# Retention rounds of a hybrid image and token network: absolute weights summed in pairs by GpSimd

## What is computed

```python
q, k = theta_shift(xn @ Wq), theta_shift(xn @ Wk)
qk = einsum("bhld,bhmd->bhlm", q, k * scaling) * mask      # 1024 x 1024 for each head
qk = qk / clip(sum(abs(qk), -1), 1, 50000)                 # row sums of absolute weights
out = einsum("bhlm,bhmd->bhld", qk, v)
out = layernorm(out) * ln_g + ln_b ; out = gelu(out) @ Wo
```

## Time and profile before

| what | value |
|---|---|
| median of 3 runs | 4394.82 us |
| lowest and highest run | 4376.67 and 4406.17 us |
| the profiled execution | 4402.8 us, its span 4401.0 us |
| mean granted TensorE clock over the span | 0.842 |
| busy over the span: PE, DVE, ACT, POOL | 72%, 62%, 40%, 35% |
| busy slices 2 to 10 of 40 (the retention stage): PE | 90% and more |

### The profile page before, as it was taken

The page is one execution under the profiler, slowest core; times in us unless marked ns, Lnnn a source line. Parts: engine busy times, 40 slices in busy tenths (PEclk is TensorE's granted clock), DMA queues, the critical chain, the costliest instruction groups (busy, mean ns, idle before and its releaser), DMA issues.

```text
span 4401.0 us, 50008 instructions
## 1 busy us (share of the span) xinstructions
PE 3157.9 (72%) x13837; PEld 1506.0 (34%) x13839; DVE 2724.1 (62%) x3838; ACT 1738.6 (40%) x3383; POOL 1533.5 (35%) x1297
## 2 busy tenths in 40 slices
PE   1899999999946637661576778757787877766648
PEld 0222222222213226651455556423343433333322
DVE  2678787788837779999655555304353443544467
ACT  0587887777835525440343444321111111100000
POOL 0111121111003458996423220253534435444500
PEclk9999999999966659995677777778988989888878
DMA  6544234442211127761011010110000000000014
GB/s 213 139 130 121 56 108 120 132 122 46 85 58 62 67 87 230 214 205 63 29 34 31 25 35 12 42 42 19 21 26 20 24 19 15 12 3 4 4 48 181
DMA packets 247369, 319.59 MB, mean 73 GB/s; under 512 B 52301, under 2 KB 183437, under 8 KB 246681
## 3 DMA queue, kind: packets, MB, share of 16 engines
q1 hardware_dynamic: 217496, 296.77, 22.1%
q0 software_dynamic: 29696, 20.97, 2.7%
HBM read 170.95 MB, written 146.67 MB: 72 GB/s over the span
## 4 chain that ended last, share of the span: by engine, by line
PE 27%; another core or an unknown queue 15%; issue 9%; DVE 9%; POOL 6%; ACT 3%; DMA 2%; SPq 0%; DVEq 0%; POOLq 0%; ACTq 0%
PE banks L1485 10%; POOL arena L903 4%; PE banks L1305 2%; PE banks L1476 2%; DVE arena L2405 2%; PE banks L1470 2%; PE banks L1365 1%; PE banks L1273 1%; ACT arena L1813 1%; DVE arena L2175 1%; POOL sorted_dram L890 1%; PE banks L1281 1%; POOL arena L916 1%; PE banks L1373 1%
## 5 line engine op out<-in xcount | busy, mean ns | idle before, releaser
L1485 PE MATMUL banks<-arena 128*128 128x512 f32 (+1 forms) x1920 | 797.2, 563 | 216.3 <-DVE arena L2586 177.1
L2586 DVE TENSOR_TENSOR arena<-arena,banks 128x1280 f32<-128x1280 f32 x320 | 465.0, 1484 | 665.6 <-remote 410.7
L1485 PEld LDWEIGHTS banks<-arena 128*128 128x128 f32 x1920 | 390.4, 205 | 682.8 <-issue 478.6
L2125 DVE TENSOR_TENSOR arena<-banks,arena 128x512 f32<-128x512 f32 x512 | 317.5, 681 | 105.2 <-PE banks L998 82.7
L812 POOL TENSOR_TENSOR pool_spare<-pool_spare 128x1 f32<-128x1 f32 x54 | 17.6, 326 | 1026.3 <-DVE edges_now L2551 717.6
L2125 DVE TENSOR_TENSOR keys<-banks,arena 128x512 f32<-128x512 f32 x512 | 317.5, 681 | 60.8 <-PE banks L998 39.0
L945 POOL DMA_INDIRECT arena<-src_dram,edges_now x336 | 317.4, 944 | 105.8 <-issue 105.8
L945 POOL DMA_INDIRECT arena<-dst_dram,edges_now x336 | 317.0, 943 | 102.4 <-issue 102.4
L2357 DVE TENSOR_TENSOR keys<-keys 128x2048 f32<-128x2048 f32 x132 | 345.7, 2658 | 2.3
L903 POOL TENSOR_TENSOR arena<-arena 128x256 f32<-128x256 f32 x144 | 337.3, 2376 | 21.8 <-ACT arena L1785 20.6
L1664 ACT ACTIVATE arena<-arena 128x512 f32<-128x512 f32 x512 | 286.8, 619 | 130.2 <-DVE arena L2125 88.5
(11 more groups left out here) (399 smaller groups left out, 5780.7 us busy)
## 6 DMA issues: line engine op xcount, KB each, us to landing
sorted_dram<-zeros SPq DMA_DIRECT2D x8, 8192.0 KB, 29.2
arena<-in_w SPq DMA_DIRECT2D x150, 384.0 KB, 4.0
arena<-parts_dram SPq DMA_DIRECT2D x192, 128.0 KB, 4.8
experts_dram<-keys SPq DMA_DIRECT2D x64, 256.0 KB
keys<-experts_dram SPq DMA_DIRECT2D x8, 2048.0 KB, 8.5
parts_dram<-nodes SPq DMA_DIRECT2D x16, 768.0 KB, 3.3
slot_out_dram<-arena SPq DMA_DIRECT2D x40, 256.0 KB, 4.4
arena<-sorted_dram SPq DMA_DIRECT2D x150, 64.0 KB, 3.3
```

Of the source, the lines that this page charges most:

```text
L1485: last = pe.matmul(banks[:, bank, 0:part.shape[1]], ohl[:, s, t, :], part, start=False, stop=False, skip_group_check=True)
L2125: dve.tensor_tensor(p_slots[r % 2][:, j, :], banks[:, j, :], table[:, PER_GROUP * g + j, at:at + HALF], ALU.mult).then_inc(masked, 1)
L2586: dve.tensor_tensor(rh[:, t % RH], oha[:, s, t:t + 1, :].broadcast_to([P, VALS, NB]), vals[:, t, :].unsqueeze(2).broadcast_to([P, VALS, NB ...
```

## The change

A new semaphore `paired` is counted by a new function of POOL. At every odd round POOL adds, head by head, the absolute tile of the even round before (`a_slots[0]`) into that of the odd round (`a_slots[1]`), in place. PE's `norm` runs only for odd rounds, and each of its four matmuls waits for its own addition and signals `norms` itself. It stands last in the index r even (after mix(r)), where it takes round r-1; the norm of round 31 stands in index 0 of the next image. ACT's Abs of an odd round waits for norm of two rounds ago, head by head; that of an even round waits for the addition of the round before, head by head. POOL's other work is put at fixed rounds behind the additions of that round, in a somewhat different order (`part_rest` before `divide` at r = 11). ACT's `part(n, 0, 1)` goes from r = 12 to 13. The semaphore `w4_in` is folded into `edges_in`, which changes no order.

```diff
@@ -249,6 +249,7 @@
         scores = sem("scores")
         masked = sem("masked")
         absolute = sem("absolute")
+        paired = sem("paired")
         norms = sem("norms")
         rot_added = sem("rot_added")
         part_step = sem("part_step")
@@ -399,7 +400,6 @@
         node_step = sem("node_step")
         vecB = sem("vecB")
 
-        w4_in = sem("w4_in")
         x3_in = [sem("x3_in_even"), sem("x3_in_odd")]
         gates_step = sem("gates_step")
         expert_ready = sem("expert_ready")
@@ -765,8 +765,8 @@
             for s in range(2):
                 load_norm(s, s)
             sp.wait_ge(rec_out, 32 * IMAGES)
-            sp.dma_start(rlast, src_dram[LAST_SRC:LAST_SRC + 1, :].broadcast_to([P, VALS])).then_inc(w4_in, 16)
-            sp.dma_start(select_in, t_in["select12"]).then_inc(w4_in, 16)
+            sp.dma_start(rlast, src_dram[LAST_SRC:LAST_SRC + 1, :].broadcast_to([P, VALS])).then_inc(edges_in, 16)
+            sp.dma_start(select_in, t_in["select12"]).then_inc(edges_in, 16)
 
             def store_experts(b):
                 for i in range(STEPS2):
@@ -837,34 +837,49 @@
                 pool.wait_ge(hn_rstd, m * (2 * PASSES) + (2 * p + 2))
                 pool.tensor_tensor(o_sb[:, p, :], o_sb[:, p, :], spread_sb[:, p % 2, :], ALU.mult).then_inc(hn_scaled, 1)
 
-            def retention(b, attend, head, tail):
-                if tail:
+            def add_pairs(b, r):
+                for j in range(PER_GROUP):
+                    pool.wait_ge(absolute, b * UNITS + r * PER_GROUP + (j + 1))
+                    pool.tensor_tensor(a_slots[1][:, j, :], a_slots[1][:, j, :], a_slots[0][:, j, :], ALU.add).then_inc(paired, 1)
+
+            def beside(b, r, attend, head, tail):
+                if r == 3 and tail:
                     divide(b - 1, 3)
                     scale_rows(b - 1, 2)
-                if head:
+                if r == 5 and head:
                     rotate_add(b + 1, 0, 0)
-                if head:
+                if r == 9 and head:
                     rotate_add(b + 1, 0, 1)
-                if attend:
-                    divide(b, 0)
-                if tail:
-                    scale_rows(b - 1, 3)
-                if head:
-                    part_rest(b + 1, 0, 0)
+                if r == 11:
+                    if head:
+                        part_rest(b + 1, 0, 0)
+                    if attend:
+                        divide(b, 0)
+                    if tail:
+                        scale_rows(b - 1, 3)
+                if r == 13 and head:
                     part_rest(b + 1, 0, 1)
-                if head:
+                if r == 17 and head:
                     rotate_add(b + 1, 1, 0)
-                if attend:
+                if r == 19 and attend:
                     divide(b, 1)
                     scale_rows(b, 0)
-                if head:
+                if r == 21 and head:
                     rotate_add(b + 1, 1, 1)
+                if r == 23 and head:
                     part_rest(b + 1, 1, 0)
-                if head:
-                    part_rest(b + 1, 1, 1)
-                if attend:
-                    divide(b, 2)
-                    scale_rows(b, 1)
+                if r == 27:
+                    if head:
+                        part_rest(b + 1, 1, 1)
+                    if attend:
+                        divide(b, 2)
+                        scale_rows(b, 1)
+
+            def retention(b, attend, head, tail):
+                for r in range(ROUNDS):
+                    if attend and r % 2:
+                        add_pairs(b, r)
+                    beside(b, r, attend, head, tail)
 
             for n in range(2):
                 for h in range(HALVES):
@@ -1014,13 +1029,12 @@
 
             def norm(b, r):
                 ps, a = divmod(r, BLOCKS)
-                if a == 0:
+                if a == 1:
                     since(pe, sum_step, b * (4 * PASSES) + (4 * ps - 3))
-                pe.wait_ge(absolute, b * UNITS + (r + 1) * PER_GROUP)
                 for j in range(PER_GROUP):
-                    last = pe.matmul(banks[ROWS * j:ROWS * (j + 1), 5, :], ones[:, 0:ROWS],
-                                     a_slots[r % 2][:, j, :], start=(a == 0), stop=(a == BLOCKS - 1))
-                last.then_inc(norms, 1)
+                    pe.wait_ge(paired, b * (UNITS // 2) + r // 2 * PER_GROUP + (j + 1))
+                    pe.matmul(banks[ROWS * j:ROWS * (j + 1), 5, :], ones[:, 0:ROWS],
+                              a_slots[1][:, j, :], start=(a == 1), stop=(a == BLOCKS - 1)).then_inc(norms, 1)
 
             def row_mean(m, p):
                 pe.wait_ge(o_ready, m * PASSES + (p + 1))
@@ -1143,13 +1157,13 @@
                         score(b, r + 1)
                     if head and r + 1 == ROUNDS:
                         score(b + 1, 0)
-                    if attend and r:
+                    beside(b, r, attend, head, tail, fresh)
+                    if attend:
+                        mix(b, r)
+                    if attend and r and r % 2 == 0:
                         norm(b, r - 1)
                     if tail and r == 0:
                         norm(b - 1, ROUNDS - 1)
-                    beside(b, r, attend, head, tail, fresh)
-                    if attend:
-                        mix(b, r)
 
             head_mean(0)
             for n in range(8):
@@ -1647,8 +1661,8 @@
                         gelu_rows(m, p)
                     elif p < 2 and attend:
                         gelu_rows(b, p)
-                if head and r in (10, 12, 22, 25):
-                    part(n, r // 20, (10, 12, 22, 25).index(r) % 2)
+                if head and r in (10, 13, 22, 25):
+                    part(n, r // 20, (10, 13, 22, 25).index(r) % 2)
                 if tail and r == 20:
                     std_of(gn_tail, gn_tail_columns, m)
                 if head and r == 25:
@@ -1660,7 +1674,10 @@
                         if attend:
                             u = r * PER_GROUP + j
                             act.wait_ge(masked, b * UNITS + (u + 1))
-                            since(act, norms, b * ROUNDS + (r - 1))
+                            if r % 2:
+                                since(act, norms, b * (UNITS // 2) + (r // 2 - 1) * PER_GROUP + j + 1)
+                            else:
+                                since(act, paired, b * (UNITS // 2) + (r // 2 - 1) * PER_GROUP + j + 1)
                             act.activation(a_slots[r % 2][:, j, :], p_slots[r % 2][:, j, :], ACT.Abs).then_inc(absolute, 1)
                         if j == 1 and r % BLOCKS == 0:
                             p = (r // BLOCKS - 1) % PASSES
@@ -2033,7 +2050,7 @@
 
             def take_sums(m, p):
                 g, qh = divmod(p, HALVES)
-                dve.wait_ge(norms, m * ROUNDS + (p + 1) * BLOCKS)
+                dve.wait_ge(norms, m * (UNITS // 2) + (p + 1) * (BLOCKS // 2 * PER_GROUP))
                 since(dve, o_ready, m * PASSES + p)
                 dve.scalar_tensor_tensor(sums, row[:, g, halves(qh)], 50000.0, banks[:, 5, :], ALU.mult, ALU.min)                    .then_inc(sum_step, 1)
                 dve.wait_ge(sum_step, m * (4 * PASSES) + (4 * p + 1))
@@ -2538,7 +2555,7 @@
             dve.wait_ge(bound_step, 4)
             dve.tensor_copy(bound[:, 1, :], banks[:, 7, 256:256 + GH]).then_inc(bound_step, 1)
             dve.wait_ge(bound_step, 5)
-            dve.wait_ge(w4_in, 16 * 2)
+            dve.wait_ge(edges_in, 32 + 16 * 2)
 
             def leaky(out, z):
                 return dve.scalar_tensor_tensor(out, z, 0.2, z, ALU.mult, ALU.max)
```

## The result

The changed kernel takes 4518.12 us in the median of its four runs (4494.64 to 4539.09), against 4391.44 for the kernel before on the same chip: ratio 1.0275, 95% interval 1.0248 to 1.0303. It is 2.75% slower; the medians lie 127 us apart. I had forecast 1.1% slower, with 4500 as the upper end: the direction was right and the size was not.

What follows compares the result with a forecast made beforehand. PE was taken as fullest engine, following ACT behind each invert. Four passes summed to 144.9 us an image against 138.1; +6.8 over seven images gave +48 us, so a median of 4442 us, range 4350 to 4500.

Steps and rivals of the forecast that it cites:

- What bounds the kernel: First-quarter stage: PE is fullest, 130.7 of 138.1 us an image, but follows ACT for a stretch behind the invert.
- the ceiling: Most the change could gain: 16 norms an image off PE, 15.5 us an image, 124 us in all.
- Additions of 1.24 us: On POOL, each new addition takes 1.24 us; four heads make 5.0 us a pair of rounds, 79 us an image.
- Chain of rounds 8 to 15: Norm(7) through Abs, additions and invert to norm(13), then index 15: the pass takes 36.8 us, before 31.7.
- Chain of rounds 0 to 7: Same chain of Abs, additions and invert up to norm(5), then index 7: the pass takes 34.5 us, before 32.0.
- Rounds 24 to 31: Four norms go (-3.9), offset by a later quantised image, slower clock and queued additions: 39.2 us against 39.3.
- the part on moved work: In rounds 24 to 31, 0.7 us added because additions of 29 stand behind `part_rest`, `divide` and `scale_rows`.
- Rounds 16 to 23: DVE sets this pass: its own 32.7 us plus 1.7 of lock waits gives 34.4, before 35.1.
- The lock: Shared SBUF access: a two-SBUF-input DVE instruction waits at most one addition, 1.24 us; r = 25 loses 4.0 instead of 1.9.
- The sum: The four passes add to 144.9 us an image against 138.1, +6.8; seven images counted, +48 us.
- The clock on top: Rival: PE about 80% busy with holes, stage clock falls to about 0.8; 4470 to 4500 us, chance 0.15.
- PE pays and nothing else does: Rival: norm(7) to norm(13) under 28 us, image about 126 us; 4299, half of it 4347; chance 0.16.

Runs made afterwards that it cites:

- e2: Changed kernel with additions over 16 of the 512 columns only, all waits and signals kept; ratio 0.9858, 4308.7 us against 4371.6 before.
- g3: Changed kernel with additions over 384 of the 512 columns, all waits and signals kept; ratio 1.0095 to the kernel before.
- f2: e1 with SyncE's 12 stack DMAs of group 1 issued after the masks of round 2 of the new image; ratio 1.0179 to the kernel before.
- e1: Changed kernel with POOL's part_rest(b + 1, 1, 1) at r = 25 instead of r = 27; ratio 1.0204 to the kernel before.
- f4: e1 with DVE's three roundings of the image at r = 26 instead of r = 25; ratio 1.0151 to the kernel before.
- f3: Kernel before with absolute tiles and ones in bf16, norm every round, no POOL additions; ratio 0.9841 to the kernel before.

## Why the prediction was right and wrong

- *What bounds the kernel.* Right: behind each invert PE follows ACT, and a norm taken away there is idle time. e2 bounds the gain: with additions of 0.22 us the whole change gives 63 us, not the 124 of the ceiling.
- *Additions of 1.24 us.* Right: shortest 1.25, median 1.28 for one, 1.23 from start to start, four in 4.94 to 4.99 where DVE takes no turn between.
- *Chain of rounds 8 to 15.* 36.8 forecast, 36.3 measured, and the parts fit as well: 29.9 us from norm(7) to norm(13). g3 shows its twelve additions. Right in kind and size.
- *Chain of rounds 0 to 7.* 34.5 forecast, 38.7 measured, 34.6 in f2, where the stacks are late. The chain was right; the step that failed is a term put at nothing: the sum lets ACT go from one image to the next without a pause, whatever the DMAs do at the loop turn. ACT stood there for 4.8 to 7.3 us. The miss is 4.2 us an image. Image 1 of the changed kernel, whose turn needs no jump back, takes 33.9.
- *Rounds 24 to 31.* 39.2 forecast, 43.1 measured, 37.9 in e1. The failed step is the part on moved work: I counted what waits on POOL and PE for `part_rest`, `divide` and `scale_rows`, but not SyncE's store and stacks behind `part_rest(1, 1)` and the score behind those. The miss is 3.9 us an image; e1 gives 5.2 back, the largest single cost that a run shows, and then the pass is 1.3 shorter than the forecast.
- *Rounds 16 to 23.* 34.4 forecast, 37.6 measured. I took DVE's busy time of 32.7 and added 1.7 of lock waits, and so put the 2.4 us that DVE stood idle in this pass at nothing, without a reason. Measured, DVE is as busy as before (32.8) and idle for 4.8. In each of the images 1 to 6 its L2015 waits 2.6 us for ACT's square root at r = 20, before 0.5; this stands on ACT behind Abs that come 1.23 apart, one for each addition of round 19. The score behind it on PE then waits 3.3 to 3.7 us for the masks instead of 1.6, and runs at the lower clock. The clock of this pass is 0.86 instead of 0.95. No run takes the wait and the clock apart, so their shares are open.
- *The lock.* 2.1 us forecast for r = 25, about 1.7 measured by duration; moving it away gains 0.9 (f4).
- *The sum.* 144.9 forecast an image, 155.7 measured by passes; 4.2 + 3.9 + 3.2 of the misses less 0.5 of rounds 8 to 15. The 138.1 of before was one image, in which rounds 8 to 15 took 31.7; in most they take 33.3, and the medians of its four passes add up to 139.8. I counted seven images; the stage grew by 128 us, eight times 16, and image 0, which I had left out, lost 16 us too. Of the 128 us, e1 gives back 29 and f2 another 24. An image of f2 takes 146.6, 6.8 more than before: just the forecast, but in part by luck, since rounds 16 to 23 lose 2.8 there where I had a gain of 0.7, and rounds 24 to 31 gain 1.5.
- *The rivals.* "The clock on top" came nearest in size, but not by its condition: it had the clock of the stage at about 0.8, and it was 0.92 (before 0.97). The lower level was granted for 129 us more; at half speed that is an estimate of 65 us of PE's work, not all of it in a chain that sets the pace. The holes before it are the waits named above. "PE pays and nothing else does" asked for less than 28 us from norm(7) to norm(13); it was 29.9. Its floor of 126 us an image is near the 129.8 that e2 reaches with additions almost free.

The first line is from before, the others from after:

```profile
628.32 0.39 PE L998 MATMUL banks<-arena 96*128 96x512 bf16 x1 [1.63 <-DVE arena L2125]
...
674.63 0.63 ACT L1681 ACTIVATE arena<-arena 128x512 f32<-128x512 f32 x1 [0.54 <-POOL keys L843]
675.86 0.63 ACT L1681 ACTIVATE arena<-arena 128x512 f32<-128x512 f32 x1 [0.60 <-POOL keys L843]
677.09 0.63 ACT L1681 ACTIVATE arena<-arena 128x512 f32<-128x512 f32 x1 [0.60 <-POOL keys L843]
677.74 1.28 ACT L1582 ACT_TABLE_LOAD   x1
679.03 0.29 ACT L1582 ACTIVATE small<-small,eps 128x1 f32<-128x1 f32 x1
...
679.36 0.16 DVE L2015 RECIPROCAL small<-small 128x1 f32<-128x1 f32 x1 [2.61 <-ACT small L1582]
```

## What to carry to other kernels

A helper engine with room in its sum can still set the pace: count how many of its new instructions stand one behind the other between two hand-overs, not its share. When work is pushed behind them, follow what it releases to the end, through the DMA queue to the first instruction that reads the data; here that was 29 of the 128 us (e1). If a matrix product costs too much only because it is f32, a narrower type for that operand may save more than moving half of it to another engine; here it gave 1.6% (f3) where the change cost 2.75%.

## What the runs showed of the hardware that I had not expected

ACT stood 2.4 to 7.3 us in the first instructions of a loop turn in six kernels, in every turn that begins with a jump back, when SyncE's stack DMAs had started 4.4 to 7.3 us ahead of the turn and kept the queues full (84% of the DMA engines' time between 715 and 760 us of the changed kernel). It did not in eight kernels whose DMAs started at most 2.9 us ahead or 8 us behind. In the profile such a wait is put down to an engine that had long been done; only the DMA records show the late packet.

PE's clock fell to its lower level behind longer holes in its work. In the changed kernel four scores take 2.40 us instead of 1.04 after an idle of 3.38 and of 5.63 us, and the granted clock is 0.50 from 684.6 to 690.7 and from 706.1 to 711.8, so the matmuls behind them take nearly twice their time too. A long hole is not needed: the level was also lower from 674.3 to 677.7, where PE had waited before many scores, but never longer than 0.34 us since 655.5.


```profile
684.63 2.40 PE L1013 MATMUL banks<-arena 96*128 96x512 bf16 x4 [3.38 <-DVE arena L2142]
...
706.13 2.40 PE L1013 MATMUL banks<-arena 96*128 96x512 bf16 x4 [5.63 <-DVE arena L2142]
```
